# A two-layer attention and feed-forward stack with its q, k and v weights loaded in two parts and its output weights kept in SBUF

## The reference

```python
def _layer(x, wqkv, qs, ksc, wo, lg, lb, w1, b1, w2, b2):
    h = shift_token(x)                      # half of the columns come from the token before
    q, k, v = split(h @ wqkv, 3)            # wqkv: 128 x 1536
    q = rotary(l2norm(q) * qs);  k = rotary(l2norm(k) * ksc)
    o = local_attention(q, k, v)            # 8 heads of 64, windows of 64 tokens
    x = x + o @ wo                          # wo: 512 x 128
    h = layernorm(shift_token(x)) * lg + lb
    a, g = split(h @ w1 + b1, 2)
    return x + (a * gelu(g)) @ w2 + b2
```

## Time and profile before

| What | Value |
|---|---|
| Median of 3 runs | 1783.23 us (1782.45 to 1784.50) |
| Profiled execution, its own time | 1786.46 us |
| Its span, from the first instruction to the last | 1784.7 us |
| Mean granted TensorE clock | 0.969 of full speed |
| TensorE (PE) busy | 1515.6 us, 85% |
| VectorE (DVE) busy | 1358.0 us, 76% |
| ScalarE (ACT) busy | 1139.9 us, 64% |
| GpSimd (POOL) busy | 1095.8 us, 61% |
| DMA: moved in all, mean rate | 112.46 MB, 63 GB/s |

### The profile page before, as it was taken

The page is one execution under the profiler, slowest core; times in us unless marked ns, Lnnn a source line. Parts: engine busy times, 40 slices in busy tenths (PEclk is TensorE's granted clock), DMA queues, the critical chain, the costliest instruction groups (busy, mean ns, idle before and its releaser), DMA issues.

```text
span 1784.7 us, 44020 instructions
## 1 busy us (share of the span) xinstructions
PE 1515.6 (85%) x15864; PEld 1233.3 (69%) x15864; DVE 1358.0 (76%) x3516; ACT 1139.9 (64%) x2364; POOL 1095.8 (61%) x1106
## 2 busy tenths in 40 slices
PE   1789999978999899977888889989998889999974
PEld 1577777766777777755666667777776777777763
DVE  6687878768787978767776479787977687979772
ACT  1576767667686767634455467676766576767671
POOL 3676868577585858623333278585857485858560
PEclk9899999989999999988999999999999999999996
DMA  8231212132221222113100132121223221212113
GB/s 284 50 122 43 57 41 62 48 95 50 68 51 48 51 71 51 40 29 122 36 25 21 46 96 54 45 54 45 63 57 87 59 60 44 54 44 54 45 28 119
DMA packets 183670, 112.46 MB, mean 63 GB/s; under 512 B 86720, under 2 KB 164128, under 8 KB 182944
## 3 DMA queue, kind: packets, MB, share of 16 engines
q1 hardware_dynamic: 183456, 109.65, 23.5%
HBM read 43.41 MB, written 23.42 MB: 37 GB/s over the span
## 4 chain that ended last, share of the span: by engine, by line
PE 50%; DVE 26%; ACT 9%; issue 7%; SPq 3%; DMA 2%; POOL 1%; DVEq 0%; ACTq 0%; POOLq 0%
PE QK L389 9%; PE TO L639 8%; PE QK L639 5%; PE TO L706 5%; DVE rope_c L1154 5%; DVE rope_s L1159 4%; DVE o_n L1179 4%; DVE top L1098 3%; PE SC L680 3%; ACT probs L1303 3%; PE TO L389 3%; PE TO L752 3%; DVE h2n L1166 3%; PE TO L808 2%; PE VB L808 2%
## 5 line engine op out<-in xcount | busy, mean ns | idle before, releaser
L1303 ACT ACTIVATE probs<-SC,shift,qgain 128x128 f32<-128x128 f32 x1024 | 390.6, 481 | 101.9 <-DVE shift L1106 101.6
L1481 POOL TENSOR_TENSOR ve<-mv,epsilon 128x1 f32<-128x1 f32 x128 | 24.5, 192 | 392.8 <-DVE mv L1145 392.8
L389 PE MATMUL QK<-w_qkv,hT 128*128 128x512 f32 x768 | 220.7, 424 | 25.5 <-DMA w_qkv<-qkv_d 12.0
L1154 DVE TENSOR_TENSOR rope_c<-QK,rope 128x512 f32<-128x512 f32 x256 | 175.7, 686 | 80.5 <-PE QK L389 78.1
L1494 POOL TENSOR_TENSOR rnorm<-clip,mhalf 128x8 f32<-128x8 f32 x128 | 211.1, 1649 | 12.4 <-DVE clip L1115 12.2
L1503 POOL TENSOR_TENSOR qgain<-clip,mhalf 128x8 f32<-128x8 f32 x128 | 209.5, 1637 | 0.0
L639 PE MATMUL TO<-ident,probs 128*128 128x128 f32 x1280 | 189.9, 276 | 12.0 <-ACT probs L1303 11.1
L1098 DVE TENSOR_REDUCE top<-SC 128x4 f32<-128x512 f32 x256 | 174.8, 683 | 31.1 <-PE SC L680 30.9
L1297 ACT ACTIVATE v_own<-VB 128x512 f32<-128x512 f32 x128 | 76.5, 598 | 189.2 <-PE VB L389 189.2
L1159 DVE TENSOR_TENSOR rope_s<-QK,rope 128x256 f32<-128x256 f32 x512 | 191.0, 415 | 0.0
L639 PEld LDWEIGHTS TO<-ident,probs 128*128 128x128 f32 x1280 | 153.8, 142 | 45.0 <-issue 24.8
(11 more groups left out here) (174 smaller groups left out, 3745.0 us busy)
## 6 DMA issues: line engine op xcount, KB each, us to landing
v_prev<-v_own SPq DMA_DIRECT2D x256, 130.0 KB, 2.3
x_att<-stream SPq DMA_DIRECT2D x128, 64.0 KB, 2.2
h<-stream SPq DMA_DIRECT2D x256, 32.0 KB, 1.9
stream<-x_new SPq DMA_DIRECT2D x32, 256.0 KB
w_qkv<-qkv_d SPq DMA_DIRECT2D x3, 1536.0 KB, 7.5
h<-x_mid SPq DMA_DIRECT2D x128, 32.0 KB
h<-x_mid SPq DMA_DIRECT2D x128, 31.8 KB
rope<-rope_d SPq DMA_DIRECT2D x24, 128.0 KB, 3.2
```

The costliest lines, as they stand in the source:

```text
L389: last = mm(dst, fr(left(a)), fr(right(b)), start=(k == 0), stop=(k == 2))
L1154: v.tensor_tensor(qk(rope_c[:])[:, m], src, rope[:, i, m, 0:1, :].to_broadcast([P, HEADS, DH]), ALU.mult)
L1303: last = nc.scalar.activation(probs[:, b, hd, :], SC[:, hd * P:hd * P + P], ACT.Exp, bias=shift[:, b, hd:hd + 1], scale=qgain[:, b, hd % 4 ...
```

## The change

The one load of `w_qkv` becomes two: `load_qk` loads the first 1024 columns of both parts (1.05 MB, two runs of 4096 bytes per partition) and `load_v` the last 512 (0.52 MB, two runs of 2048 bytes). At the change of layers the first waits for the last k product (`s_k`) and the second for the last v product (`s_v`) of the old layer; both hooks stand at place 2, where `after_qkv` stood. v has a semaphore of its own, `s_vw`, and TensorE waits for it before the v product of the first tile of a sequence, from the second layer on. `w_o` gets room for both layers, is loaded once at the start by one DMA, and `after_wo` and the load between the stacks go. TensorE waits for it once per stack.

```diff
-        w_o = sb("w_o", [P, PAIRS, DIM])
+        w_o = sb("w_o", [P, DEPTH, PAIRS, DIM])
...
+        s_vw = sem("s_vw")
...
-            def load_qkv(l):
-                sp.dma_start(w_qkv[:], qkv_d[l]).then_inc(s_qkvw, 16)
-
-            def load_wo(l):
-                sp.dma_start(w_o[:], wo_in[l].rearrange("(c p) n -> p c n", p=P)).then_inc(s_wow, 16)
+            def load_qk(l):
+                sp.dma_start(w_qkv[:, :, 0:1024], qkv_d[l, :, :, 0:1024]).then_inc(s_qkvw, 16)
+
+            def load_v(l):
+                sp.dma_start(w_qkv[:, :, 1024:1536], qkv_d[l, :, :, 1024:1536]).then_inc(s_vw, 16)
...
                 if k == 0:
-                    load_wo(0)
+                    sp.dma_start(w_o[:], wo_in.rearrange("l (c p) n -> p l c n", p=P)).then_inc(s_wow, 16)
...
-                def after_qkv():
+                def after_qk():
+                    wait_tile(s_k, m + TILES - 1)
+                    load_qk(1)
+
+                def after_v():
                     wait_tile(s_v, m + TILES - 1)
-                    load_qkv(1)
-
-                def after_wo():
-                    wait_tile(s_y, m + TILES - 1)
-                    load_wo(1)
-
-                iteration(SEQS, [(0, rope_after(5)), (1, rope_after(6)), (2, after_qkv), (2, rope_after(7)), (6, after_wo)],
+                    load_v(1)
+
+                iteration(SEQS, [(0, rope_after(5)), (1, rope_after(6)), (2, after_qk), (2, after_v), (2, rope_after(7))],
                           lambda: load_ffn(1))
...
-            load_qkv(0)
-            load_wo(0)
+            load_qk(0)
+            load_v(0)
...
                     if t := tile(WO):
-                        if t.i == 0:
-                            pe.wait_ge(s_wow, t.loads() * 16)
+                        if t.c == 0:
+                            pe.wait_ge(s_wow, 16)
...
-                            last = mm(OB[:, 0:DIM], oT[:, c, :], w_o[:, c, :], start=(c == 0), stop=(c == PAIRS - 1))
+                            last = mm(OB[:, 0:DIM], oT[:, c, :], w_o[:, t.c // TILES // SEQS, c, :], start=(c == 0), stop=(c == PAIRS - 1))
...
+                        if t.i == 0:
+                            need(pe, s_vw, (t.loads() - 1) * 16)
                         product(mm, VB[:], lambda x: hT[:, b, x, :], lambda x: w_qkv[:, x, 1024:1536]).then_inc(s_v, 1)
```

## The result

The changed kernel takes 1772.9 us (median of five runs, 1771.40 to 1775.83) against 1783.23 for the kernel before on the same chip: ratio 0.9941, 95% interval 0.9926 to 0.9956, so 7.8 to 13.2 us less. The forecast was 1774.2. The profiled execution took 1771.4 us, its span is 1769.6.

The account below looks back on a forecast made before the run. TensorE held half the chain of waits, with stalls for `w_qkv` and `w_o` at layer changes. 2.6 + 2.8 + 4.4 = 9.8 us off gave 1773.4 on the median, plus 0.8: 1774.2 us; range 1770.0 to 1778.2.

Parts of the forecast that it names:

- SP's queue, not the weights in use, sets the moment of the load: At layer changes, SP's in-order queue accounts for 5.6 us between last v product and load; q and k issue unchanged.
- q and k 1.3 us sooner: At each layer change, the smaller q and k load lands 1.3 us sooner; 2.6 us in all.
- my bound of 2.8: Upper bound on the first change's gain: a third of the whole landing, if all of it shrinks with the bytes.
- v in time: At layer changes, v lands near 393.3, over 1 us before its product is due; cost nothing.
- The wait for `w_o` goes and nothing replaces it: At output products after layer changes, the 2.55 us waits go; steps shorten by 2.8 and 4.4 us.
- The rival of GpSimd's hidden chain: The `w_o` wait hid GpSimd's own chain, so steps keep their length; 1781.5 us, 7 in 100.
- The clock still falls in the shorter stall: At layer changes, TensorE's clock still falls to 1.2 GHz; the 2.1 us cost at each stays.
- the rival of a clock that stays up: The clock no longer falls at one or both changes, 2.1 us less each; 1772.1 or 1770.0, 10 in 100.
- The start costs nothing: At the start, the added 0.26 MB fits a 1.8 us gap of the DMA engines; cost nothing.
- The bound that I had written for it: Upper bound on the start's cost: 0.9 us if the DMA engines' gap is gone.
- half of the slow clock behind `w_o`: Behind the `w_o` wait, 1.5 us of slow clock stands in one of two rows; half counted, 0.8 us given back.

Follow-up runs that it names:

- e4: The changed kernel with both the q and k load and the v load one step earlier in SP's list; ratio to the kernel before 0.9917.
- e5: The changed kernel with q, k and v loaded as one DMA, one step earlier in SP's list; ratio to the kernel before 0.9894.
- e2: The kernel before with only the output weights of both layers kept; q, k and v still one load at the old place; ratio 0.9944.
- e1: The kernel before with only the q, k and v load split; output weights loaded and waited for as before; ratio 0.9985, 2.7 us.
- e7: The changed kernel with the q and k load one step earlier and the v load left in place; ratio to the kernel before 0.9907.
- e9: The changed kernel with q and k loaded one step earlier and layer 1's v weights in their own buffer, loaded a sequence earlier; 1759.4 us, ratio 0.9859.
- e10: e9 with layer 1's output weights loaded in the second sequence, not at the start; 1760.5 us, ratio to the kernel before 0.9867.

## Why the prediction was right

- **SP's queue, not the weights in use, sets the moment of the load.** Right: issued at the old place, 5.0 us after the step's first move; e4 and e5 show it by moving the place.
- **q and k 1.3 us sooner.** Right in sum: 1.5 us a change over twelve stalls, 2.7 us for the split alone. Wrong for each stall: I said 5.7 and 3.7 us and they were 4.07 and 4.51. At the first change I had taken off a third of the load's slow end (one DMA engine alone), but the whole of that end went, and the gain was 3.0 us in this pair, above my bound of 2.8, and 2.3 over all traces. At the second it was 0.5 and 0.7. That the two errors cancel is luck.
- **v in time.** Right: there 1.4 us before its product (I said over 1). SP needs 0.62 us and not 0.43 for each of the two strided loads, so v goes out 0.66 us behind. The section of the Trainium skill that I cited ("DMA: Bandwidth & Descriptors", on the anatomy of one DMA) fits its 2 us to DMAs issued by GpSimd, and here SP issues. A fixed cost of that size isn't paid in series here: v landed 1.3 us behind q and k, the time of its bytes, and not 3.3.
- **The wait for `w_o` goes and nothing replaces it.** Right: steps of 9.13 and 9.20. The rival of GpSimd's hidden chain has fallen.
- **The clock still falls in the shorter stall.** Right: both new stalls end in products of 2.93 us. Its price at these stalls was too high, 1.2 us where I read 2.1 from the steps; it entered the sum on neither side, and only the rival of a clock that stays up rested on it.
- **The start costs nothing.** This step failed. I put the added bytes into the idle 1.8 us of the DMA engines before 31.9 and took the inputs ahead of them as untouched. `b_1raw`, issued 1.5 us before them, took 0.6 us longer to land, and everything behind it moved: 0.9 us with the 0.2 us that lay in its issue. The bound that I had written for it was the measured value, though it was worked out from the rate of the engines and not from this delay.

The sum with what was measured: 3.0 for the split, 2.9 + 4.4 for `w_o` in this pair, less 0.9 for the start, 9.4 us, and 0.8 less if half of the slow clock behind `w_o` is given back; measured 10.3, interval 7.8 to 13.2. The steps of the two traces give more for the changes, 12.1 us, since this execution of the kernel before had the longest stall of all. What the runs cannot settle is the rest of about 1 us, and whether the stretch between the stacks gained too: single executions of the kernel before ran from 1779 to 1791 us over the study, and from the first move to that of tile 31, a stretch in which no kernel of the study has a stall for a weight, the twelve traces have 326.6 to 332.2 us.

## What to carry to other kernels

When a transfer is late, look first at what stands between its condition and its issue in the issuing engine's list; here that was 5.6 of the 14 us between the last old product and the first new one, and moving the whole load by one step won more (some 9 us, e5 against e2) than shrinking the hurried part by a third (2.7 us, e1). A bulk load moved ahead of small urgent moves makes these the next wait, so take bytes out of the hurried load (keep what fits, load it a stage earlier) rather than only reorder. Bytes added to a saturated start can delay what stands ahead of them; here the delay shows in the traces of the start but not in the whole time, in which the kernels with the lighter start were no faster beyond the intervals.

## What the runs showed of the hardware

- A load issued later delayed one issued 1.5 us earlier: with 0.26 MB more behind it, `b_1raw` took 5.68 us on the mean of eight traces (5.19 to 6.04) and not 5.05 (four traces, 4.73 to 5.34).
- Behind 1.57 MB just issued, SP was held 2.00 to 5.11 us in issuing a DMA of one row (four cases, e4 and e5; 3.76 in the one shown) whose median is 0.8 us; behind 1.05 MB, 1.20 to 2.82 us (six cases, e7, e9 and e10). A bulk load thus delays not only the landings but the issues behind it.
- Of two idle times of 2.55 us of TensorE one left the granted clock at 1.00 and one at 0.69; in e1 one of 2.24 us left it at 1.00 and one of 3.43 at 0.69. Behind each of the eight of 4.0 to 5.0 us the six products took 2.4 to 2.9 us in place of 1.65.
